# Second expert weights partly loaded in the last attention period, biases prepared early and added in two row tiles

## The reference, cut to what matters

```python
logits = xn @ gate_w_moe + gate_b_moe
tw, ti = jax.lax.top_k(logits, K)                 # K = 2 of E = 8
tw = jax.nn.softmax(tw, axis=-1)
h = jax.nn.gelu(jnp.einsum('bsd,edf->besf', xn, w1) + b1[None, :, None, :], approximate=False)
eo = jnp.einsum('besf,efd->besd', h, w2) + b2[None, :, None, :]
moe = jnp.einsum('besd,bse->bsd', eo, wdense)
```

## Time and profile before

| | |
|---|---|
| median of 3 runs | 3228.68 us (3226.07 to 3230.05) |
| the profiled execution | 3223.67 us, its span 3222.0 us |
| TensorE busy | 2843.5 us (88%) |
| VectorE, ScalarE, GpSimd busy | 2137.2, 1439.1, 1266.2 us |
| stages | attention 221 to 1357, experts 1357 to 2000, joining to 2150, state-space to the end |

### The profile page before, as it was taken

One profiled execution on the slowest core, in us unless ns is written; L12 is line 12 of the kernel. 1 busy time (PEld: TensorE's weight loads), 2 busy tenths in 40 slices (PEclk: granted clock), 3 DMA queues, 4 the chain that ended last, 5 costly groups with the idle time before them and its releaser, 6 DMA issues.

```text
span 3222.0 us, 44752 instructions
## 1 busy us (share of the span) xinstructions
PE 2843.5 (88%) x14054; PEld 1323.5 (41%) x14055; DVE 2137.2 (66%) x2953; ACT 1439.1 (45%) x2500; POOL 1266.2 (39%) x1425
## 2 busy tenths in 40 slices
PE   6788898898898988689999998888899999999986
PEld 4455433333233332156667665762222332332222
DVE  7577486686776865022222222655999999999997
ACT  4431365565565666611212211425445455545442
POOL 3230021221221222200000001835889888888895
PEclk9899998898999989889999999898899898998978
DMA  6655313313132130131111112730000000000000
GB/s 209 176 144 162 120 28 59 48 41 59 30 60 47 28 51 24 57 106 30 32 32 30 33 29 65 225 112 7 1 14 20 1 20 20 1 20 14 1 14 20
DMA packets 175001, 176.38 MB, mean 55 GB/s; under 512 B 50641, under 2 KB 151508, under 8 KB 174716
## 3 DMA queue, kind: packets, MB, share of 16 engines
q1 hardware_dynamic: 168700, 157.52, 19.8%
q0 software_dynamic: 6144, 16.82, 1.6%
HBM read 100.46 MB, written 73.83 MB: 54 GB/s over the span
## 4 chain that ended last, share of the span: by engine, by line
PE 52%; DVE 16%; POOL 11%; issue 9%; ACT 3%; DMA 2%; SPq 1%; POOLq 0%; DVEq 0%; ACTq 0%
PE ps L1724 49%; DVE hh L1690 6%; POOL Ch L915 5%; DVE mp L1460 5%; DVE ps L1677 2%; PE ps L1974 2%; POOL yg L814 1%; DMA qk<-qk_parts 1%; ACT Pt L1065 1%; PE ps L1925 1%; POOL dt L881 1%; SPq L625 1%; DVE tl L1667 1%; POOL dtx L875 1%; ACT dA L1245 1%
## 5 line engine op out<-in xcount | busy, mean ns | idle before, releaser
L1460 DVE TENSOR_REDUCE mp<-ps 128x1 f32<-128x1024 f32 (+7 forms) x768 | 669.1, 909 | 258.6 <-PE ps L1724 247.6
L1065 ACT ACTIVATE Pt<-ps 128x512 f32<-128x512 f32 (+3 forms) x1280 | 609.5, 539 | 345.1 <-PE ps L1724 339.6
L1724 PE MATMUL ps<-qk 99*128 99x512 bf16 (+7 forms) x2560 | 632.9, 359 | 88.7 <-DVE mp L1460 42.8
L915 POOL TENSOR_TENSOR Ch<-hh,Cb 128x1024 f32<-128x1024 f32 x256 | 603.9, 2361 | 40.6 <-DVE hh L1690 40.6
L774 POOL TENSOR_SCALAR_AFFINE_SELECT Pt<-Pt 128x128 f32<-128x128 f32 x512 | 146.8, 292 | 859.5 <-ACT Pt L1065 851.8
L1690 DVE TENSOR_TENSOR_SCAN hh<-dA,hst,ps 128x512 f32<-128x512 f32 x384 | 472.9, 1262 | 0.0
L1724 PEld LDWEIGHTS ps<-qk 99*128 99x128 bf16 (+1 forms) x2560 | 212.1, 99 | 544.3 <-DVE mp L1460 190.4
L1245 ACT ACTIVATE dA<-ps 128x1024 f32<-128x1024 f32 x256 | 261.5, 1022 | 349.5 <-PE ps L1724 348.5
L1724 PE MATMUL ps<-dtx,pick 32*128 32x512 f32 x1024 | 329.6, 690 | 70.1 <-DVE hh L1690 69.3
L1677 DVE TENSOR_TENSOR ps<-ps,Bb 128x512 f32<-128x512 f32 x512 | 325.5, 680 | 27.0 <-PE ps L1724 26.7
L1724 PE MATMUL ps<-dt,WA 32*128 32x512 f32 x1024 | 325.5, 715 | 13.2 <-ACT dA L1245 12.3
(11 more groups left out here) (305 smaller groups left out, 3520.7 us busy)
## 6 DMA issues: line engine op xcount, KB each, us to landing
qk<-qk_parts SPq DMA_DIRECT2D x192, 128.0 KB, 6.2
W<-in_L_ffn_w SPq DMA_DIRECT2D x16, 1024.0 KB, 11.9
qk_parts<-q SPq DMA_DIRECT2D x32, 384.0 KB, 2.9
expert_out<-yb SPq DMA_DIRECT2D x72, 128.5 KB, 2.5
expert_in<-zero SPq DMA_DIRECT2D x9, 1024.0 KB, 10.5
xg<-expert_in SPq DMA_DIRECT2D x72, 128.0 KB, 2.8
X<-in_L_attn_x SPq DMA_DIRECT2D x2, 2048.0 KB, 10.3
x_rows<-x2h SPq DMA_DIRECT2D x8, 512.0 KB, 5.0
```

Of the source, the lines that this page charges most:

```text
L915: pool.tensor_tensor(Ch[:, k % 6, :, :], hh[:, k % HRING, :, :], Cb[:, par:par + 1, :].broadcast_to([P, 2, CH]), ALU.mult).then_inc(s_Ch, 1)
L1065: act.activation(Pt[:, n % PRING, q0:CH], ps[:, 4 + n % SRING, q0:CH], ACT.Exp, scale=SCALE).then_inc(s_exp, 1)
L1460: dve.tensor_reduce(mp[:, qc, h, t % TPC, k0 // 1024:k0 // 1024 + 1], slot[:, 0:n], AX.X, ALU.max).then_inc(s_free, 1)
L1724: return pe.matmul(o, lhsT, rhs, start=start, stop=stop, **kw)
```

## The change: early weights, early biases, row tiles

W2's experts 1 to 4 lie where qk0 lay, and their loads are issued in SyncE's program ahead of the last period, once the products of period 6 are done; 0, 5, 6 and 7 follow after the barrier, and b2b behind them. b1 is loaded in the first attention period, into two buffers of Pt, as two halves of 512 columns at partitions 0 to 23 and 32 to 55. VectorE makes there the three bf16 parts, now each in its eight rows of a half, and pickb as one column for each block. In the expert stage GpSimd copies a block's column to `pcur`, and TensorE takes that column, broadcast to 128, as weights of two matmuls of 24 rows, one in the row tile at 0 and one at 32, which write the two halves. They stand together ahead of the products.

```diff
@@ SyncE
             load_group(1, 1)
             load_v(0)
+            sp.wait_ge(s_bz, 1)
+            for j in range(2):
+                for a in range(3):
+                    sp.dma_start(bt[32 * j + E * a:32 * j + E * a + E, :], b1[:, j * CH:(j + 1) * CH]).then_inc(s_b, 16)
...
             period(NG - 2, 0, FULL_PLAN, NM + (NG - 2) * NR, True, False)
+            def load_w2(experts):
+                for e in experts:
+                    sp.dma_start(W2[:, e, :, :], w2[e, :, :].rearrange("(k p) f -> p k f", p=P)).then_inc(s_ew2, 16)
+            sp.wait_ge(s_pv, (NG - 1) * STEPS + 2)
+            load_w2(range(1, 5))
             period(NG - 1, 1, LAST_PLAN, NM + (NG - 1) * NR, False, False)
             sp.wait_ge(s_aod, 16 * (NG * CPB + 1))
             stage_end(sp, 2)
-            sp.wait_ge(s_bz, 1)
-            for a in range(3):
-                sp.dma_start(bt[32 * a:32 * a + E, :], b1).then_inc(s_b, 16)
-            sp.dma_start(b2b[:, :, :], b2.rearrange("(a e) n -> a e n", a=1).broadcast_to([P, E, D])).then_inc(s_b, 16)
...
             load_block(0, 0)
             load_block(1, 1)
-            for e in range(E):
-                sp.dma_start(W2[:, e, :, :], w2[e, :, :].rearrange("(k p) f -> p k f", p=P)).then_inc(s_ew2, 16)
+            load_w2((0, 5, 6, 7))
+            sp.dma_start(b2b[:, :, :], b2.rearrange("(a e) n -> a e n", a=1).broadcast_to([P, E, D])).then_inc(s_b, 16)
@@ GpSimd, attention
             pool.memset(zero[:, :, :], 0.0).then_inc(s_zero, 1)
             pool.wait_ge(s_zero, 2)
+            pool.memset(bt, 0.0).then_inc(s_bz, 1)
+            pool.wait_ge(s_bz, 1)
+            po.link(pool.iota(rid[:, 0:1], pattern=[[0, 1]], base=0, channel_multiplier=1))
+            pool.sem_inc(s_bz, 1)
@@ GpSimd, experts
-            pool.memset(bt[:, :], 0.0).then_inc(s_bz, 1)
-            po.link(pool.memset(row_e[:, :], -1.0))
-            for e in range(E):
-                for a in range(3):
-                    po.link(pool.affine_select(out=row_e[:, :], in_=row_e[:, :], compare_op=ALU.not_equal, fill=float(e),
-                                               base=-32 * a - e, pattern=[[0, 1]], channel_multiplier=1))
-            pool.sem_inc(s_bz, 1)
+            def expert_rows(i, par):
+                pool.wait_ge(s_hid, i + 1)
+                pool.tensor_copy(pcur[0:64, par:par + 1], pickb[0:64, ds(i, 1)]).then_inc(s_pick, 1)
+            with pool.Fori(0, NBLK // 2) as i:
+                for par in range(2):
+                    expert_rows(i * 2 + par, par)
@@ VectorE, first attention period
+            def expert_biases():
+                h = slice(0, 64)
...
+                dv.mark(dve.tensor_scalar(pickb[:, :], eid[:, :], rof[:, 0:1], None, ALU.is_equal))
+                for a in (1, 2):
+                    dv.link(dve.tensor_copy(b3[h, :], (bt, br)[a - 1][h, :]))
+                    dv.link(dve.scalar_tensor_tensor(out=br[h, :], in0=b3[h, :], scalar=rof[h, a:a + 1], in1=(bt, br)[a - 1][h, :],
+                                                     op0=ALU.mult, op1=ALU.add))
+                dve.tensor_copy(b3[h, :], br[h, :]).then_inc(s_pick, 1)
             ring(0, None, 0, FIRST_PLAN)
+            expert_biases()
             dve.wait_ge(s_fev, 2)
@@ VectorE, experts
-            dve.wait_ge(s_b, 64)
-            dve.wait_ge(s_bz, 2)
-            dv.link(dve.tensor_copy(b3[:, :], bt[:, :]))
...
-            dve.tensor_copy(pickb[:, :, :], pick[:, :].rearrange("p (i a) -> p i a", a=1).broadcast_to([P, NBLK, P])).then_inc(s_pick, 1)
+            dve.wait_ge(s_b, 7 * 16)
@@ TensorE, hidden
                 pe.wait_ge(s_gelu, i + 1)
+                pe.wait_ge(s_pick, i + 2)
+                for j in range(2):
+                    r = slice(32 * j, 32 * j + 3 * E)
+                    mm(ps[:, 2 * par + j, :], pcur[r, par:par + 1].broadcast_to([3 * E, P]), b3[r, :], True, False, tile_position=(32 * j, 0))
                 for j in range(2):
                     o = ps[:, 2 * par + j, :]
-                    mm(o, pickb[:, ds(i, 1), :].rearrange("p a n -> p (a n)"), b3[:, j * 512:(j + 1) * 512], True, False)
                     for k in range(KD):
```

More of the change, by code:

```diff
@@ L267, in build @@
         wpj = sb("wpj", [P, KD, D], at=m0)
+        b3 = sb("b3", [P, DF // 2], BF16, at=m0)
+        pickb = sb("pickb", [P, NBLK], BF16, at=m0)
+        rid = sb("rid", [P, 4], I32, at=m0)
+        pcur = sb("pcur", [P, 2], BF16, at=m0)
+        rof = sb("rof", [P, 4], at=m0)
         m1 = ExitStack()
@@ L337, in build @@
         zero = sb("zero", [P, 1, D], at=m2)
+        bt, br = Pt[:, 0, :], Pt[:, 1, :]
         qs, ks = [[t[:, w, :, :] for t in (qk0, qk1)] for w in range(2)]
@@ L344, in build @@
         b2b = sb("b2b", [P, E, D], at=m4)
[L345 to L348, removed]
         xg = sb("xg", [P, 2, D], at=m4)
@@ L351, in build @@
         hg = sb("hg", [P, 2, DF], at=m4)
-        br, bt = hg[:, 0, :], hg[:, 1, :]
         hT = sb("hT", [P, 2, KF, P], at=m4)
@@ L1487, in ring @@
                         dve.wait_ge(s_free, base + (r + 1))
+            def expert_biases():
+                h = slice(0, 64)
+                dve.wait_ge(s_b, 6 * 16)
+                dve.wait_ge(s_bz, 2)
+                dv.mark(dve.tensor_single_scalar(rid[:, 1:2], rid[:, 0:1], E - 1, ALU.bitwise_and))
+                dv.link(dve.tensor_single_scalar(rid[:, 2:3], rid[:, 0:1], 31, ALU.bitwise_and))
+                dv.mark(dve.tensor_copy(rof[:, 0:1], rid[:, 1:2]))
+                dv.mark(dve.tensor_scalar(rof[:, 1:2], rid[:, 2:3], float(E), -1.0, ALU.is_ge, ALU.mult))
+                dv.link(dve.tensor_scalar(rof[:, 2:3], rid[:, 2:3], float(2 * E), -1.0, ALU.is_ge, ALU.mult))
+                dv.mark(dve.tensor_scalar(pickb[:, :], eid[:, :], rof[:, 0:1], None, ALU.is_equal))
[4 more added lines that the diff above has]
+                dve.tensor_copy(b3[h, :], br[h, :]).then_inc(s_pick, 1)
             ring(0, None, 0, FIRST_PLAN)
+            expert_biases()
             dve.wait_ge(s_fev, 2)
```

## The result

| | before | changed |
|---|---|---|
| median of 8 runs, us | 3227.76 (3223.08 to 3230.05) | 3215.70 (3209.95 to 3221.29) |
| ratio | | 0.9967, 95% interval 0.9957 to 0.9976 |
| profiled execution, us (span) | 3223.67 (3222.0) | 3221.29 (3219.6) |
| first matmul of the loop after attention's last store of `ao` | 36.37 | 19.33 |
| a block of the loop | 8.412 | 8.499 |

By the ratio the kernel is faster by 10.7 us (7.8 to 13.9); 3217.8 was predicted. The profiled execution of the changed kernel is the slowest of its 8 runs, so the two traces are compared by stages and not by their spans. Attention's last store is at 1354.61 before and at 1359.69 after, and from the first gather to the end the changed kernel takes 1222.9 us instead of 1219.4.

The account below looks back on a forecast made before the run. The expert stage was taken as bound by the wait for second weights at its start, then by TensorE's instructions in 71 blocks. Terms -18 + 7.1 = -10.9 us gave 3217.8 us from a median of 3228.68, range 3210 to 3228.

Parts of the forecast that it names:

- The start: Start of the expert stage: with half the second weights already loaded, the loop starts at 1372.9 instead of 1390.98, gaining 18 us.
- the release: Barrier ahead of the expert stage: SyncE arrives last, goes at 1357.0 and issues the first weight load at 1357.9.
- the first load: First 1 MB of second weights behind the barrier: lands 4.8 us after issue; up to 3 us more would make the gain 15.
- The first block: TensorE's first expert block: begins at 1359.8, takes 9.14 us, is done at 1369 with 4 us in hand before the weights.
- The tiles: Bias matmuls of each expert block in row tiles: 0.53 us against 0.43, +0.10 a block, +7.1 us over 71 blocks.
- What was costed at nothing: VectorE's moved bias instructions (at most 5 us, hidden), moved loads, early weight loads and GpSimd's copy: 0; contention 0 to 1 us.
- GpSimd's copy: Copy of 64 values in each expert block, awaited by TensorE: 0.19 us with some 8 us of time, so 0.
- A: Rival, expert blocks: tiles cost no pause, both bias matmuls in 0.22 us, 14.9 us won, total 3195.8 us; chance 0.05.
- B: Rival, expert blocks: tiles don't run at once and pauses are paid, +0.32 us a block, total 3233.4 us; chance 0.08.
- C: Rival: start gains only 15 us or blocks lose up to 13.5, total 3223 to 3224 us; chance 0.17 together with D.
- D: Rival: early loads delay the last attention period, losing part of the 18 us; chance 0.17 together with C.
- the bound of 0.19 us a block: Upper bound in the expert blocks: broadcast column loaded as weights at f32's price, bias piece 0.62 us, +13.5 us in all.

Follow-up runs that it names:

- x4: Changed kernel with all eight experts' second weights loaded behind the barrier, none early: 3230.13 us, ratio 1.0006.
- x5: Changed kernel with two experts' second weights loaded early instead of four: 3267.64 us in one run on a second chip, where the kernel before took 3276.47.
- x3: Kernel before with only the early loads of experts 1 to 4 added, bias work unchanged: 3221.26 us, ratio 0.9976.
- x6: Changed kernel with each bias matmul directly ahead of its own half's products, two tile visits a block: 3298.01 us, one run on a second chip.
- x7: Changed kernel with both bias matmuls in the same row tile, so they can't run at once: 3283.90 us, one run on a second chip.
- x2: x1 without GpSimd's copy, TensorE reading the block's column directly from pickb: 3206.36 us, ratio 0.9934 against the kernel before.
- x1: Changed kernel with bias matmuls over all 128 rows, zeros outside their own, no row tiles: 3206.48 us, ratio 0.9933 against the kernel before.
- x8: x2 plus three unneeded f32 matmuls while TensorE waits for the second weights: 3253.82 us on a third chip, ratio 0.9945 against the kernel before.

## Why the prediction was right

**The start.** 18 us were forecast (18.08 from the prediction's own times) and 17.04 measured. Of the 1.04 us less, 0.34 is the release (first load issued 3.63 us after the store instead of 3.29): the prediction had SyncE as the last to arrive at the barrier, and the chain of waits names GpSimd, which came 5.59 us after its last mask in both kernels. The other 0.7 is the first load, which took 5.49 us to land instead of 4.8; the three behind it came 3.0 us apart, as forecast (14.50 us from the first issue at 1363.32 to the last landing instead of 13.8). The first block had 3.38 us in hand (4 forecast), b2b 3.4 us (3.0 forecast: 1375.9 to 1378.9), and the weights stayed last. That the start depends on the loads alone is shown by x4 and x5; that the bias work would have taken their place, by x3.

**The tiles.** +0.10 us a block was forecast and +0.087 measured, 6.2 us for 71 blocks instead of 7.1. The sum of 0.22 for both tiles and twice 0.10 of pause and 0.10 of load, read from f32 tiles of another stage, holds for bf16 tiles of 24 rows too, to 0.01 us, and x6 and x7 show that it is a sum: one visit more costs one visit's price. The two errors, 1.0 and 0.9 us, went against each other: the stage is 11.02 us shorter where 10.9 was forecast. That the sum is this close is in part luck.

**What was costed at nothing.** VectorE's eleven instructions are hidden with 14.9 us left. The last attention period, from the last store of the period ahead of it to its own last store, takes 95.46 us after 95.40, and 95.46 in x3. In x4, without early loads, it takes 94.14, and x4's own rival had named a shorter period there as a sign of harm. But TensorE's waits in it are the same in all four traces (11.6 us for ScalarE), and the clock is not: in x4 it is 1.00 from 8 us into the period up to its last 8, while the other three, the kernel before among them, which has no early load, show two stretches of 8 us at 0.87 and 0.91 to 0.92. So no wait for the early loads shows; whether they have a part in the clock there is open. GpSimd's copy takes this, and is waited for by nobody:

```profile
L814 POOL COPY pcur<-pickb x72: 179/179/183, 1362.6 to 1962.8; 64x1 bf16 x72
```

(ns, least, median, most). It has 8.3 us of time in each block, and x2 without it is as fast as x1.

**The rivals.** A, no pause: block 8.499, not 8.2. Its first half is true, the tiles do run at once (0.39 us for both), and its second is false. The rule of the Trainium skill on packed matmuls ("TensorE: Matmul & The Clock Gate", Part 3), one matmul and 4 ns for each further tile, gives an estimate of 0.22 us for the piece. The Trainium skill's "TensorEngine Tiling (Array Packing)", Key Properties, says that a change of tiling mode drains the engine; with the changed kernel's block and those of x6 and x7 the runs side with this one. B, tiles one after the other with the pauses paid: x7 is that case, at +0.299 a block (forecast +0.32), and the changed kernel isn't it. C would need 0.13 us a block with a start that gains 15, or 0.19 a block; D needs a delay of over 30 us for the scatter. Neither is there.

**What the steps missed.** No step asked what the tiles were for. The pass saved by running both at once is 0.22 us, the visit costs 0.30, and the same selection by zeros over all rows, at 0.43 us, was open all the time: x2 is 0.33% below the changed kernel by the ratios. Of that the stage shows 6.9 us: 6.2 in the blocks, 1.2 from the clock at its end, and some tenths lost at its start. The ratios differ by 10.7 us, but their intervals are 6 and 9 us wide, so I hold to the stage. Something more may lie behind it: from the first gather to the end the five kernels with row tiles take 1220.4 to 1227.2 us and the five without 1219.3 to 1220.1, each in one execution, in code that is the same. What makes that, and whether it is the tiles, is open.

## What to carry over

Where two chains end a few us apart, changing one wins little: here 4.7 and 4.8 us alone and 17.0 together. The profile of before says so for the first of them, since it shows the first block done at 1386.08, 4.90 us ahead of the loop. Count visits to row tiles as well as the columns saved in them: a visit costs 0.30 us here, so it must save more than that, and rows that are zero cost nothing: a bf16 matmul of 512 columns takes 0.22 us with 24 rows and with 128. A wait of TensorE also costs the clock behind it; look at the granted clock of the stretch after a wait before the wait is priced by its length.

## What was not expected

- The clock: after 3.2 us and more of idle time the loop's first piece took 5.65 to 6.82 us instead of 4.04, 1.9 us more at the same work in the kernel before against x3 (5.95 and 4.04), 2.8 more in x5 (6.80), of which its tiles are 0.1. In the kernel before the clock fell during the wait; in the changed kernel it was still 1.00 through its 3.38 us and fell within the loop's first us (0.89 in the mean from 1378.75 to 1379.75, then 0.50). After 2.52 us at the stage's end it fell in some executions and not in others.
- In the changed kernel the first block of the stage took 10.89 us (1364.75 to 1375.64) instead of the 9.14 from before, though nothing in it got longer but the tiles: more of it ran at half clock, which rose 7.9 us after the block's first matmul instead of 4.3. Neither the earlier beginning nor the tiles explain that: x1 and x2 begin as early and take 9.28 and 9.27, and x8, without tiles, takes 10.00. What decides when the clock rises is open. It used up part of the margin that I had counted on.
- A broadcast bf16 column as weights is loaded at the price of an ordinary matrix: 98 ns in 128 rows, as the matrix of before, and 91 ns in 24. Here the columns are one value repeated, and the bound of 0.19 us a block that I had kept for it was not needed.
